# A routed front, a selective-scan mixer and a slotted expert stage in one kernel: routing order, scan entry and gate positions changed

## The chip, the cores and the metric

One NeuronCore of a Trainium2 chip runs the whole kernel. Its engines are TensorE (PE in the rows, with PEld for its weight loads), VectorE (DVE), ScalarE (ACT), GpSimd (POOL) and SyncE (SP), which here only issues DMAs. The metric is the device time of one execution in microseconds, as the median of several runs.

## The reference

A block on `x` of shape (2, 1024, 256) with a conditioning vector per batch row:

```python
c = cond(x, t_emb)            # shared SwiGLU + 8 gelu experts of width 128, top 2 by a sigmoid router, / 3
y_f = mamba(c, forward weights); y_b = flip(mamba(flip(c), backward weights))
g = sigmoid([y_f, y_b] @ gate_w + gate_b)
x = x + (g * y_f + (1 - g) * y_b) @ proj_w + proj_b
z = cond2(x, random)          # per channel: softmax over time of 2|x|/sum|x|, cumulative sum,
                              # count of sums <= random picks a time, x kept where |x| >= |x[time]|
x = x + ffn(z)                # 64 experts x 32 slots: soft dispatch over the batch, one 256x256 layer each, soft combine
```

The mixer is a Mamba layer with 512 inner channels and 16 states: a projection to `u` and `z`, a causal convolution of 4 taps and silu on `u`, a projection of it to step, B and C, `delta = softplus(dt @ dt_w + dt_b)`, and then

```python
h = exp(delta_t * A) * h + (delta_t * u_t) * B_t ;  y_t = sum_n h * C_t      # over 1024 times
y = (y + u * D) * silu(z) ;  return y @ outproj
```

## The kernel before

**Stages.** `moe_phase` computes the routed front (and folds the convolution's taps into the projection's weights on GpSimd beside it), `mamba_phase` the scan, `mix_phase` the gates, projection and thresholds, `ffn_phase` the experts. Each stage is a block in which every engine has its own program, written out by hand; semaphores order them, and nothing is reordered by a compiler. An engine works strictly in the order of its program. The products of the front and the last stage are made of three fp32r products of high and low parts (`split_products`, line 32 in the rows).

**Routing.** A unit `g` is one block of 128 hidden rows on 512 tokens: `value(g)` and `factor(g)` on TensorE into a ring of three banks, `hidden(g)` (silu or gelu) on ScalarE, `product(g)` on VectorE, `high_hidden(g)` and `low_hidden(g)` the two parts on ScalarE and VectorE, `project(g)` on TensorE. Units 0 to 3 of each 12 are the shared layer, the other eight are experts, whose factor is a gate. In the first tokens' units the router's logits are computed as well, and a chain of small VectorE operations turns them into gates: `rank`, `mask`, `den`, `rden`, `comb`, and at its end `comb_ready`. `turn_gates` on TensorE waits for it. GpSimd makes the low parts of the weights and tokens, one after the other in the order of `SPLITS`; those of the second expert weights, `rw2`, are numbers 6 and 7.

**Scan.** Four groups (2 batch rows x 2 directions) `k`, each of four channel blocks `p`: 16 periods `w` of 16 units `s`. A unit is 128 lanes (32 channels x 4 states) x 1024 times. For each, ScalarE makes `exp(delta * A)` into one of two slots of `hs` (`decay`, L1212; L1203 in the first four), GpSimd the input `dbu` (L1287), VectorE the scan (L1374) and the product with C (L1388, `weigh`), which GpSimd does for units 0, 4, 8 and 12 of most periods (L1293); TensorE sums the states of four units (`add_states`, L1087, L1080 at the very end) onto `skip`, the product with D. `hc` has six slots, `dbu` four. After unit 1 of the next period `gate_out` (L1354) multiplies the sum with `silu(z)`.

Beside this, each period makes what the next one needs: the step `t` (`step_size`, two halves of 512 times), copied by ScalarE in `step_in` (L1160, L1161), then exponential and logarithm (L1174, L1178), all ahead of a DMA that spreads it over the lanes; `z_gate` and ScalarE's `gate` (L1194), which needs another table of functions than the exponentials, so a table load before and after; and for the next group the projection `u` with its convolution and silu (`conv`, L1131). All small products share two PSUM banks in turn, in the order of `bank_uses`: a product waits until the bank's last reader is through. `pe_chores` gives TensorE's order at each quarter `r` of a period; `STEP_AT`, `GATE_AT`, `CONV_AT` and so on give the units after which ScalarE does its pieces, `LATE_STEP_AT` in the last period of a group.

**Entry into the scan.** For the first group the convolution isn't folded: ScalarE copies `u` (L1136, L1137), VectorE applies three taps (L1398), ScalarE the silu (L1142), TensorE the projection to rows of step, B and C (L966). The rows go to DRAM and come back spread over the lanes. The first four units get their step and input from PSUM by products with a spreading matrix (L999, L1009), and `replica` (L1185) copies the inputs.

**Mix.** Per batch row and channel half: magnitudes and shares on ScalarE, then on VectorE the cumulative sum (L1799) and three passes for the threshold.

## Time and profile before

| | us |
|---|---|
| runs | 1465.29, 1465.84, 1461.80; median 1465.29 |
| profiled execution | 1465.12 |
| its span | 1463.3 |
| PE busy | 1178.0 |
| DVE busy | 1150.0 |
| POOL busy | 884.2 |
| ACT busy | 771.5 |

The stages follow each other with a fence between: the front to about 184 us, the scan to 1060, the mix to 1121, the experts to the end. A row of the order of time gives start, duration, engine, line, operation, tiles and number of instructions merged into it; in brackets stands the idle time of the engine ahead of it and who ended it.

### The profile page before, as it was taken

What the parts mean: (1) busy time and instruction counts of PE and PEld (TensorE: products, weight loads), DVE (VectorE), ACT (ScalarE), POOL (GpSimd) and SP (SyncE); (2) the same over time, 40 slices, a digit from 0 to 9 for tenths busy, and PEclk for the clock granted to TensorE, in tenths of its full rate; (3) what the DMA queues carried; (4) which work ended last, traced back from release to release, by engine and by line L of the source; (5) the groups of instructions that cost most, each with busy time, mean ns of one, the idle gap of its engine ahead of it and who ended that gap; (6) DMA issues with size and microseconds to landing.
All of it is one profiled execution on the core that took longest, in us unless ns stands there. A gap on an engine that the chain in (4) does not pass through costs nothing. (4 is left out here: it accounts for less than half of the span.)

```text
span 1463.3 us, 14748 instructions
## 1 busy us (share of the span) xinstructions
PE 1178.0 (81%) x4924; PEld 651.5 (45%) x4924; DVE 1150.0 (79%) x1052; ACT 771.5 (53%) x1031; POOL 884.2 (60%) x394
## 2 busy tenths in 40 slices
PE   6999986787649887469887466484499999999998
PEld 4788732232113332113322122131147788787887
DVE  4444469999999999999999999999977754545445
ACT  5444465777545776555775555465246534333330
POOL 4420028999999999999999999999910000000000
PEclk9999998998859899769999588687699999999999
DMA  5353235341463234345123337313014130303012
GB/s 202 113 175 134 78 121 207 130 172 72 162 230 147 95 132 157 118 189 201 72 98 137 145 128 295 142 59 115 0 60 170 51 125 1 144 0 129 0 35 80
DMA packets 46016, 176.34 MB, mean 121 GB/s; under 512 B 5873, under 2 KB 10481, under 8 KB 33538
## 3 DMA queue, kind: packets, MB, share of 16 engines
q1 hardware_dynamic: 45954, 175.57, 32.7%
q8 instruction: 32, 0.52, 0.1%
q14 instruction: 30, 0.25, 0.1%
HBM read 142.78 MB, written 32.77 MB: 120 GB/s over the span
## 5 line engine op out<-in xcount | busy, mean ns | idle before, releaser
L1287 POOL TENSOR_TENSOR scan_dbu<-scan_rep,scan_bc 128x1024 f32<-128x1024 f32 x254 | 592.6, 2361 | 33.4 <-ACT scan_rep L1185 26.0
L1374 DVE TENSOR_TENSOR_SCAN scan_hs<-scan_hs,scan_dbu 128x1024 f32<-128x1024 f32 x191 | 436.7, 2286 | 11.3 <-ACT scan_hs L1212 9.9
L1212 ACT ACTIVATE scan_hs<-scan_rep,scan_neg_a 128x1024 f32<-128x1024 f32 x252 | 280.7, 1118 | 305.7 <-DVE scan_hc L1388 279.9
L1087 PE MATMUL scan_ysum<-scan_hc,scan_sel 128*32 128x512 f32 x1008 | 172.9, 818 | 210.1 <-DVE scan_hc L1388 200.0
L1388 DVE TENSOR_TENSOR scan_hc<-scan_hs,scan_bc 128x1024 f32<-128x1024 f32 x191 | 233.5, 1223 | 6.1
L1087 PEld LDWEIGHTS scan_ysum<-scan_hc,scan_sel 128*32 128x32 f32 x1008 | 36.1, 131 | 324.1 <-issue 276.0
L1293 POOL TENSOR_TENSOR scan_hc<-scan_hc,scan_bc 128x1024 f32<-128x1024 f32 x65 | 153.2, 2357 | 12.7 <-DVE scan_hc L1374 12.3
L1374 DVE TENSOR_TENSOR_SCAN scan_hc<-scan_hs,scan_dbu 128x1024 f32<-128x1024 f32 x65 | 148.1, 2278 | 0.8 <-POOL scan_dbu L1287 0.7
L947 PE MATMUL banks<-late_xin,scan_inwf 128*128 128x512 f32 x256 | 115.6, 606 | 0.0
L32 PE MATMUL ffn_sl<-ffn_tanh_s,xm_s 128*128 128x512 f32 x384 | 107.2, 415 | 2.3 <-DVE ffn_tanh_s L2169 2.3
L1989 PE MATMUL ffn_oy<-ffn_y,ffn_et 128*128 128x256 f32 x448 | 102.0, 379 | 0.8 <-DVE ffn_y L2216 0.8
L1989 PEld LDWEIGHTS ffn_oy<-ffn_y,ffn_et 128*128 128x128 f32 x448 | 84.9, 190 | 13.5 <-DVE ffn_y L2216 1.3
L32 PE MATMUL banks<-phi_s,xt_s 128*128 128x512 f32 x336 | 85.3, 400 | 0.7 <-PEq L1461 0.7
L947 PEld LDWEIGHTS banks<-late_xin,scan_inwf 128*128 128x128 f32 x256 | 48.4, 193 | 69.7 <-issue 69.7
L32 PE MATMUL moe_second<-moe_hid_s,moe_w_s 128*128 128x512 f32 x288 | 73.6, 391 | 5.2 <-DVE moe_hid_s L459 5.2
L32 PEld LDWEIGHTS ffn_sl<-ffn_tanh_s,xm_s 128*128 128x128 f32 x384 | 70.0, 190 | 16.3 <-DVE ffn_tanh_s L2169 3.3
L2084 ACT ACTIVATE ffn_lsb<-banks 128x512 f32<-128x512 f32 x56 | 33.4, 596 | 65.2 <-PE banks L32 63.8
L32 PEld LDWEIGHTS banks<-phi_s,xt_s 128*128 128x128 f32 x336 | 60.9, 188 | 13.9 <-issue 2.4
L2178 DVE TENSOR_TENSOR ffn_tanh<-ffn_lsb 128x512 f32<-128x512 f32 x24 | 16.6, 692 | 61.2 <-ACT ffn_lsb L2084 61.2
L32 PEld LDWEIGHTS moe_second<-moe_hid_s,moe_w_s 128*128 128x128 f32 x288 | 53.5, 188 | 18.3 <-DVE moe_hid_s L459 5.8
L32 PE MATMUL moe_first<-moe_x_s,moe_w_s 128*128 128x512 f32 x240 | 60.0, 391 | 0.4 <-POOL moe_w_s L417 0.4
L2075 ACT ACTIVATE ffn_et<-ffn_tb 128x512 f32<-128x512 f32 x32 | 19.0, 594 | 76.4 <-PE ffn_tb L2021 76.4
(277 smaller groups left out, 1805.3 us busy)
## 6 DMA issues: line engine op xcount, KB each, us to landing
scan_rep<-dd_rows SPq DMA_DIRECT2D x60, 1024.0 KB, 5.6
scan_bc<-bc_rows SPq DMA_DIRECT2D x32, 512.0 KB, 5.9
ffn_wt<-in_ew SPq DMA_DIRECT2D x16, 1024.0 KB, 8.0
dd_rows<-scan_dd SPq DMA_DIRECT2D x15, 1024.0 KB, 3.8
scan_bc<-gate_rows SPq DMA_DIRECT2D x24, 256.0 KB, 4.8
scan_inwf<-fold SPq DMA_DIRECT2D x12, 512.0 KB, 3.8
cond<-scan_bc SPq DMA_DIRECT2D x16, 256.0 KB, 3.0
y_all<-scan_yo SPq DMA_DIRECT2D x6, 512.0 KB, 3.1
```

What stands on the lines that cost most here:

```text
L32: mm = nc.tensor.matmul(out, lhs[x], rhs[y], start=first and i == 0, stop=last and i == 2)
L947: mm = nc.tensor.matmul(out, inwf[:, q % IWR, c, t, :], xin[k % 2][:, c, h * CT + t:h * CT + t + CT], start=(t == 0 and c == 0), stop=(t = ...
L1087: mm = nc.tensor.matmul(ysum[i * D32:(i + 1) * D32, h, :], sel[:], hc[:, (s0 + i) % HCR, h * CT:(h + 1) * CT], start=False, stop=last, til ...
L1212: nc.scalar.activation(hs[:, s % HSR, :], rep[:, e % REPS, 0, :], ACT.Exp, scale=scale).then_inc(da_done, 1)
L1287: nc.gpsimd.tensor_tensor(dbu[:, s % DBR, :], rep[:, e % REPS, 1, :], bc[:, j, 0, :], ALU.mult).then_inc(dbu_done, 1)
L1293: nc.gpsimd.tensor_tensor(hc[:, s % HCR, :], hc[:, s % HCR, :], bc[:, s % UPP // NI, 1, :], ALU.mult).then_inc(pool_hc_done, 1)
L1374: nc.vector.tensor_tensor_scan(states, hs[:, s % HSR, :], dbu[:, s % DBR, :], 0.0, ALU.mult, ALU.add).then_inc(scan_done, 1)
L1388: nc.vector.tensor_tensor(hc[:, s % HCR, :], hs[:, s % HSR, :], bc[:, r // NI, 1, :], ALU.mult).then_inc(hc_done, 1)
L1989: mm = nc.tensor.matmul(bank[:, b * DM:(b + 1) * DM], et[:, b, j, m * P:(m + 1) * P], y[:, j, b, :], start=(j == 0), stop=(j == JT - 1))
L2075: nc.scalar.activation(et[:, 0, :, m * P:(m + 1) * P], tb[:].rearrange("p (j s) -> p j s", j=JT), ACT.Copy).then_inc(et_act, 1)
L2084: nc.scalar.activation(lsb[:, m % 2, b, :], lg[:, (m + 1) % 2 if first else b, :], ACT.Copy).then_inc(l_copied, 1)
L2178: nc.vector.tensor_tensor(tanh[:], lsb[:, m % 2, 1, :], first_logits[:, m, :] if first else lsb[:, m % 2, 0, :], ALU.subtract).then_inc(di ...
```

## The change

Six things, in order of the program:

- In the routing TensorE makes five products of zeros (`IDLE_PRODUCTS`) after the first small product. On VectorE `low_hidden(2)` and `product(3)` go ahead of `mask`; on GpSimd the splits of `rw2` wait for `comb_ready`. `turn_gates` goes ahead of `value(5)`, `factor(4)` ahead of `value(6)`. ScalarE loads the silu table before the last `output`.
- The entry into the scan: the last channel block is convolved and activated in two halves; each half goes on to its projection, its copy (half 0 on ScalarE, half 1 on VectorE), its step. B rows for units 0 to 3 are spread by TensorE into `hs` slot 1 (`spread_rows`) and copied into `bc` by ScalarE, so one DMA less brings them. The input of unit 1 is spread into `ysum` and used from there. GpSimd does `weigh(0)` ahead of its inputs; `skip(0, 0)` comes after the spreads; the exponential of `neg_a` comes after the steps.
- In each period `z` comes ahead of `skip`, but in the last period of a group and the very first; `gate` comes at unit 3 instead of 4, or at 6 in those last periods (`LATE_GATE_AT`); 7 in the very first stays.
- The step's exponential and logarithm both come at unit 2 (before: 2 and 3), or 4 (before: 5).
- For periods 1 and 2 of a group's channel blocks (`split_step`) the second half of the step product moves from the end of one period into the start of the next, behind the sums. The late sigmoids go from units 9 and 14 to 10 and 15.
- In the mix each cumulative sum follows its own share.

```diff
+            pe.wait_ge(padded, 1)
+            for _ in range(IDLE_PRODUCTS):
+                zeros = comb_wide[:].rearrange("p t e -> p (t e)")
+                nc.tensor.matmul(by_expert, zeros[:, 0:P], zeros, start=True, stop=True)
...
             project(2)
+            turn_gates()
             value(5)
             project(3)
-            turn_gates()
+            factor(4)
             value(6)
-            factor(4)
...
             high_hidden(NC * UNITS - 1)
+            nc.scalar.preload_act_table_set("silu_and_others")
             output(NC - 1)
...
                 pool.wait_ge(high_done, s + 1)
+                if s == RW1:
+                    pool.wait_ge(comb_ready, 1)
...
             product(2)
+            low_hidden(2)
+            product(3)
             link(nc.vector.tensor_scalar(mask[:], rank[:], float(TOP_K), None, ALU.is_lt))
...
-            low_hidden(2)
-            product(3)
...
+def split_step(k, p):
+    return k + 1 < GROUPS and p in (1, 2)
+def gates_late(k, p):
+    return p == DC - 1 or (k, p) == (0, 0)
...
-        return [(*key, h) for key in step for h in range(HALVES)] + [("skip", k, p)] + [("z", k, p, h) for h in range(HALVES)]
+        split = [("t", k, p + 1, 1)] if split_step(k, p) else []
+        gate, own = [("z", k, p, h) for h in range(HALVES)], [("skip", k, p)]
+        return [(*key, h) for key in step for h in range(HALVES)] + split + (own + gate if gates_late(k, p) else gate + own)
...
-    step = [(*key, h) for key in step for h in range(HALVES)] if r == NJ - 1 else []
+    step = [(*key, h) for key in step for h in range(1 if split_step(k, p + 1) else HALVES)] if r == NJ - 1 else []
...
-STEP_AT = (1, 2, 3)
-LATE_STEP_AT = (3, 5, 5)
-GATE_AT, FIRST_PERIOD_GATE_AT = 4, 7
+STEP_AT = (1, 2, 2)
+LATE_STEP_AT = (3, 4, 4)
+GATE_AT, LATE_GATE_AT, FIRST_PERIOD_GATE_AT = 3, 6, 7
...
-FIRST_GATE_AT = {9: 0, 14: 1}
+FIRST_GATE_AT = {10: 0, 15: 1}
...
+            def spread_rows(h):
+                freed(pe, ("x", 0, h))
+                pe.wait_ge(consts_in, 3 * 16)
+                nc.tensor.matmul(hs[:, 1, h * CT:(h + 1) * CT], spread[0:XROWS, NI * P:], dbl[:, h * CT:(h + 1) * CT],
+                                 start=True, stop=True).then_inc(spread_done, 1)
...
+                if i == 1:
+                    for h in halves:
+                        mm = nc.tensor.matmul(ysum[:, h, :], spread[:, i * P:(i + 1) * P], dd[:, 1, h * CT:(h + 1) * CT],
+                                              start=True, stop=True)
...
+                act.wait_ge(spread_done, h + 1)
+                nc.scalar.activation(bc[:, 0, 0, h * CT:(h + 1) * CT], hs[:, 1, h * CT:(h + 1) * CT], ACT.Copy).then_inc(uc0_done, 1)
...
+                    if s == DVE_INPUTS:
+                        weigh(0)
...
+                    nc.vector.tensor_tensor_scan(cum[:, cc, :], ones[:], share[:, cc, :], 0.0, ALU.mult, ALU.add).then_inc(chain, 1)
+                    links[0] += 1
                 each(b, lambda cc, s: nc.vector.reciprocal(s[:, 1:2], s[:, 3:4]))
-                each(b, lambda cc, s: nc.vector.tensor_tensor_scan(cum[:, cc, :], ones[:], share[:, cc, :], 0.0,
-                                                                   ALU.mult, ALU.add))
```

TensorE's program in the routing, from project(1) to project(4): L32 into `moe_second` is a `project`, L32 into another tile a `value` or `factor`, L244 / L250 `turn_gates`, L284 / L290 an expert's factor. Before:

```order
L32 MATMUL moe_second<-moe_hid_s,moe_w_s 128x512 x6
L32 MATMUL moe_first<-moe_x_s,moe_w_s 128x512 x6
L32 MATMUL moe_second<-moe_hid_s,moe_w_s 128x512 x6
L32 MATMUL moe_first<-moe_x_s,moe_w_s 128x512 x6
L32 MATMUL moe_second<-moe_hid_s,moe_w_s 128x512 x6
L244 MATMUL moe_first<-moe_ident,moe_comb_wide 32x128 x16
L32 MATMUL banks<-moe_x_s,moe_w_s 128x512 x6
L284 MATMUL moe_first<-moe_gates_s,moe_ident_s 128x512 x4
L284 MATMUL banks<-moe_gates_s,moe_ident_s 128x512 x2
L32 MATMUL moe_second<-moe_hid_s,moe_w_s 128x512 x6
```

And of the change:

```order
L32 MATMUL moe_second<-moe_hid_s,moe_w_s 128x512 x6
L32 MATMUL moe_first<-moe_x_s,moe_w_s 128x512 x6
L32 MATMUL moe_second<-moe_hid_s,moe_w_s 128x512 x6
L250 MATMUL moe_first<-moe_ident,moe_comb_wide 32x128 x16
L32 MATMUL moe_first<-moe_x_s,moe_w_s 128x512 x6
L32 MATMUL moe_second<-moe_hid_s,moe_w_s 128x512 x6
L290 MATMUL moe_first<-moe_gates_s,moe_ident_s 128x512 x2
L32 MATMUL banks<-moe_x_s,moe_w_s 128x512 x6
L290 MATMUL moe_first<-moe_gates_s,moe_ident_s 128x512 x2
L290 MATMUL banks<-moe_gates_s,moe_ident_s 128x512 x2
L32 MATMUL moe_second<-moe_hid_s,moe_w_s 128x512 x6
```

`turn_gates` has moved up by a value and a project, and the first factor stands one value earlier.

TensorE's program at the border of the scan's periods 1 and 2: L947 / L980 is the folded projection, L983 / L1027 the step, L1087 / L1139 the sums, L1059 / L1111 `skip`, L1024 / L1076 `z`. Before:

```order
L947 MATMUL banks<-late_xin,scan_inwf 128x512 x8
L983 MATMUL banks<-scan_dbl,scan_dtw 128x512 x2
L1087 MATMUL scan_ysum<-scan_hc,scan_sel 32x512 x8
L1059 MATMUL scan_ysum<-late_uc,scan_diag 128x512 x2
L1024 MATMUL banks<-scan_xin,scan_inwz 128x512 x4
L1087 MATMUL scan_ysum<-scan_hc,scan_sel 32x512 x8
```

And of the change:

```order
L980 MATMUL banks<-late_xin,scan_inwf 128x512 x8
L1027 MATMUL banks<-scan_dbl,scan_dtw 128x512
L1139 MATMUL scan_ysum<-scan_hc,scan_sel 32x512 x8
L1027 MATMUL banks<-scan_dbl,scan_dtw 128x512
L1076 MATMUL banks<-scan_xin,scan_inwz 128x512 x4
L1111 MATMUL scan_ysum<-late_uc,scan_diag 128x512 x2
L1139 MATMUL scan_ysum<-scan_hc,scan_sel 32x512 x8
```

One half of the step now stands behind the sums, and `z` ahead of `skip`.

ScalarE's program from unit 0 of the scan's period 1: L1212 / L1270 is the exponential, L1160 and L1161 / L1214 and L1215 the step's copies, L1174 and L1178 / L1228 and L1232 its exponential and logarithm, L1194 / L1252 the gate. Before:

```order
L1212 ACTIVATE scan_hs<-scan_rep,scan_neg_a 128x1024
L1174 ACTIVATE scan_dd<-scan_dd 128x1024
L1212 ACTIVATE scan_hs<-scan_rep,scan_neg_a 128x1024
L1178 ACTIVATE scan_dd<-scan_dd 128x1024
L1212 ACTIVATE scan_hs<-scan_rep,scan_neg_a 128x1024
L1194 ACT_TABLE_LOAD
L1194 ACTIVATE scan_sz<-banks 128x512 x2
L1253 ACT_TABLE_LOAD
L1212 ACTIVATE scan_hs<-scan_rep,scan_neg_a 128x1024 x4
```

And of the change:

```order
L1270 ACTIVATE scan_hs<-scan_rep,scan_neg_a 128x1024
L1228 ACTIVATE scan_dd<-scan_dd 128x1024
L1232 ACTIVATE scan_dd<-scan_dd 128x1024
L1270 ACTIVATE scan_hs<-scan_rep,scan_neg_a 128x1024
L1252 ACT_TABLE_LOAD
L1252 ACTIVATE scan_sz<-banks 128x512 x2
L1316 ACT_TABLE_LOAD
L1270 ACTIVATE scan_hs<-scan_rep,scan_neg_a 128x1024 x5
```

The logarithm and the gate each stand one exponential earlier.

## Rows read from the trace of the kernel before

**Rows 1.** The page: busy time, and two groups of the scan
```profile
PE 1178.0 (81%) x4924; PEld 651.5 (45%) x4924; DVE 1150.0 (79%) x1052; ACT 771.5 (53%) x1031; POOL 884.2 (60%) x394
...
L1212 ACT ACTIVATE scan_hs<-scan_rep,scan_neg_a 128x1024 f32<-128x1024 f32 x252 | 280.7, 1118 | 305.7 <-DVE scan_hc L1388 279.9
...
L1388 DVE TENSOR_TENSOR scan_hc<-scan_hs,scan_bc 128x1024 f32<-128x1024 f32 x191 | 233.5, 1223 | 6.1
```

**Rows 2.** PE's 40 slices on the page; one stretch of the scan, columns PE to POOL
```profile
PE   6999986787649887469887466484499999999998
...
600.00:700.00 100.00, 66.53 (x219) 22.17 (x218) 97.47 (x56) 58.10 (x62) 98.10 (x44) 0.78 0.50 184
```

**Rows 3.** Order of time, TensorE, start of the routing
```profile
12.07 4.82 PE L32 MATMUL banks<-moe_x_s,moe_w_s 128*128 128x512 f32 x12 [8.05 <-DVE moe_w_s L443]
...
34.65 1.64 PE L32 MATMUL moe_second<-moe_hid_s,moe_w_s 128*128 128x512 f32 x6 [2.28 <-DVE moe_hid_s L459]
...
38.57 1.66 PE L32 MATMUL moe_second<-moe_hid_s,moe_w_s 128*128 128x512 f32 x6 [0.92 <-DVE moe_hid_s L459]
...
43.29 1.15 PE L284 MATMUL moe_first<-moe_gates_s,moe_ident_s 128*128 128x512 f32 x4 [0.47 <-issue]
...
46.23 1.62 PE L32 MATMUL moe_second<-moe_hid_s,moe_w_s 128*128 128x512 f32 x6 [1.31 <-DVE moe_hid_s L459]
```

**Rows 4.** Order of time, VectorE, the chain that makes the gates
```profile
29.00 1.74 DVE L486 TENSOR_SCALAR moe_mask<-moe_rank 128x128 f32<-128x128 f32 x1
30.77 2.36 DVE L487 TENSOR_TENSOR moe_comb_wide<-moe_prob,moe_mask 128x128 f32<-128x128 f32 x1
...
37.62 0.29 DVE L499 TENSOR_TENSOR moe_comb_wide<-moe_comb_wide,moe_mask 128x128 f32<-128x128 f32 x1
```

**Rows 5.** Order of time, entry into the scan
```profile
187.58 1.28 ACT L1230 ACT_TABLE_LOAD   x1
...
190.20 7.14 PE L956 MATMUL banks<-scan_xin,scan_inwf 128*128 128x512 f32 x16 [0.50 <-ACT late_uc L1137]
...
191.50 12.11 DVE L1398 SCALAR_TENSOR_TENSOR late_uc<-scan_hc,scan_taps,late_uc 128x1024 f32<-128x1024 f32 x9 [1.11 <-ACT late_uc L1137]
...
215.57 1.22 DVE L1366 TENSOR_TENSOR scan_dbu<-banks,scan_bc 128x1024 f32<-128x1024 f32 x1 [2.42 <-DMA scan_bc<-bc_rows]
...
228.09 2.35 POOL L1293 TENSOR_TENSOR scan_hc<-scan_hc,scan_bc 128x1024 f32<-128x1024 f32 x1
...
235.20 2.30 DVE L1374 TENSOR_TENSOR_SCAN scan_hs<-scan_hs,scan_dbu 128x1024 f32<-128x1024 f32 x1
...
253.69 2.30 DVE L1374 TENSOR_TENSOR_SCAN scan_hs<-scan_hs,scan_dbu 128x1024 f32<-128x1024 f32 x1 [1.07 <-POOL scan_dbu L1287]
```

**Rows 6.** VectorE's waits, 230 to 1070 us: total us, times, longest
```profile
DVE scan_hs L1374 <- ACT scan_hs L1212: 9.9, 18, 2.2
...
DVE late_uc L1354 <- PE scan_ysum L1087: 1.9, 2, 1.1
...
DVE wide L1354 <- PE scan_ysum L1087: 1.1, 1, 1.1
```

**Rows 7.** Order of time, ends of period 1: TensorE's sums, ScalarE's gate
```profile
314.05 1.92 PE L1087 MATMUL scan_ysum<-scan_hc,scan_sel 128*32 128x512 f32 x16 [1.43 <-DVE scan_hc L1388]
...
328.13 3.64 PE L1087 MATMUL scan_ysum<-scan_hc,scan_sel 128*32 128x512 f32 x16
...
340.20 1.08 ACT L1194 ACTIVATE scan_sz<-banks 128x512 f32<-128x512 f32 x2
```

**Rows 8.** Order of time: GpSimd's last gap, its inputs 248 to 251, scan 249
```profile
918.47 2.36 POOL L1293 TENSOR_TENSOR scan_hc<-scan_hc,scan_bc 128x1024 f32<-128x1024 f32 x1 [0.31 <-DVE scan_hc L1374]
...
1027.14 9.33 POOL L1287 TENSOR_TENSOR scan_dbu<-scan_rep,scan_bc 128x1024 f32<-128x1024 f32 x4
...
1033.52 2.27 DVE L1374 TENSOR_TENSOR_SCAN scan_hs<-scan_hs,scan_dbu 128x1024 f32<-128x1024 f32 x1
```

**Rows 9.** Order of time, VectorE in the mix, second batch row
```profile
1101.25 4.47 DVE L1799 TENSOR_TENSOR_SCAN scan_bc<-mix_ones,scan_bc 128x1024 f32<-128x1024 f32 x2
```

117 lines of the change are left out of this document (72 added, 45 removed).

## The prediction

> **What bounds the kernel now.** The page comes first: no engine is busy all the time, TensorE 81%, VectorE 79%, GpSimd 60% [rows 1], in a span of 1463.3 us. The slices and one stretch say why: there are three stages with different bounds [rows 2]. In the routing stage TensorE is at 9 tenths or more from the second slice of 36.6 us to the fifth, and so again in the last ten slices; in the scan between (217 to 1059 us) VectorE is at 97.47 of 100 and GpSimd at 98.10, with TensorE's granted clock at 0.78, that is part of the time at 1.2 instead of 2.4 GHz. The change touches the start of the routing stage, the entry into the scan, the order inside the scan's 16 periods, and one place in the mix between scan and last stage. So the third view is the order of time at these places, read for the gap of the engine that bounds the stage, since only that gap can be won, and the fourth is the list of VectorE's waits inside the scan.
>
> **Routing, first 47 us.** TensorE's work there is fixed; what can go is its gaps, 2.28 + 0.92 + 0.47 + 1.31 = 4.98 us, and slow matmuls [rows 3]. The gaps wait for the chain of small VectorE operations that ends in `comb_ready`. In it a 128x128 mask takes 1.74 us and a 128x128 product 2.36, where the same size takes 0.29 a little later [rows 4]: the long ones lie beside GpSimd's splits. The change puts `low_hidden(2)` and `product(3)` ahead of the chain and holds GpSimd's split of the second expert weights until `comb_ready`. My walk: project(2)'s operand is ready at 30.4, when TensorE is still in value(4), so the 2.28 goes; the chain starts at 31.1 instead of 29.0, but its eleven links now take 3.1 us, so `comb_ready` comes at 34.2 instead of 37.9; the gate transposes meet it with 0.3 us of waiting, and project(4) starts at 42.4 instead of 46.23 after one gap of about 1.0. So 4.98 - 0.3 - 1.0 = 3.7 us. What is late next: the held splits, 2 x 2.4 us from 34.2, end at 39 and are needed at 42.4.
> The first twelve products take 4.82 us [rows 3], where six take 1.62 and less later on: they run at the lower clock after an empty stretch of 8 us. The five products of zeros go ahead of them, in a gap of 8.05 us; they are ten instructions of such a kind as take 7.14 / 16 = 0.45 us at the higher clock [rows 5], so at half of it they would end near 13, 1 us too late, at worst. If the clock has risen midway they end near 10.4 and cost nothing. Then value(0) ends at 13.5; factor(0) waits for GpSimd's split until 14.2, and 16.82 - 15.6 = 1.2 us is won. Bounds: -1 and 1.9. Routing: **4.9 us** (2.7 to 6.9).
> The trace agrees with a rule of the Trainium skill ("SBUF — State Buffer", Who interferes with whom): a VectorE operation with two SBUF inputs and a GpSimd one block each other whole. By it the links cost what they cost alone, as I took. The skill's "TensorE: Matmul & The Clock Gate" (Part 1) has the slow state as the default that activity releases; whether zeros are activity enough no row shows.
>
> **Entry into the scan.** The table load of 1.28 us stands between ScalarE's second and third copies [rows 5] and goes to a place where ScalarE idles; VectorE's taps for the second channel block start 191.50 -> 190.75, 0.7 us. The last taps are cut in two halves (0.8 us more work), but projection, step and softplus of the first half run beside the second. B rows no longer pass through DRAM for unit 0: the 2.42 us wait for them goes; instead two more TensorE products and two ScalarE copies. My walk puts scan(0) at 213.8 instead of 215.57 + 1.22 = 216.8. Unit 1's product comes straight from PSUM, scan(1) at 217.4. GpSimd does weigh(0) first, not after inputs(3) (2.35 us) [rows 5]. Not all arrives: ScalarE now has the step's copies, exponential and logarithm ahead of decay(5), so scan(5) starts at 232.9 instead of 235.20, 2.3 us. The 1.07 us that scan(10) waits for GpSimd goes too, since that engine started 4.8 us earlier. **3.4 us** (1 to 5: below if the copies of B make decay(0) late, above if ScalarE catches up). `skip(0,0)` moves behind the spreads and is hidden: its first reader needs product 3.
>
> **Inside the scan.** VectorE waits for ScalarE's exponentials 18 times, 9.9 us, and for TensorE's sum at the period's end 1.9 + 1.1 us in three periods [rows 6]: 12.9 us, all that can be won. Why: after exponential r (1.12 us) [rows 1] the gate costs 1.28 + 1.08 + 1.28, the next exponential 1.12, together 5.9 us. From the release of exponential r to scan r+1 VectorE has two pairs of scan (2.3) and product (1.2), 6.9 us; but 5.8 if GpSimd makes one of the products, as at unit 4. There the gate ends late, mostly by 0.35 us. At unit 3 both products are VectorE's and a microsecond is over. In last periods of a group the gate waited for its product (2.24 us once); at unit 6 that is long done. Elsewhere z now precedes skip and no longer waits for VectorE's gate_out. The two sigmoid pairs move from 9 and 14 to 10 and 15, away from GpSimd's units 11 and 13.
> The three gate_out waits: in periods 1 and 2 of a group the second half of the step product waited for a bank behind a ScalarE convolution and held the sums, which then took 3.64 us at the lower clock, 1.92 at the higher [rows 7]. The split puts it behind the sums.
> What comes back: (a) in those six periods ScalarE's second step copy now waits for that half. At the higher clock the half is there in time; at the lower one it comes at about 331.2 where ScalarE wanted it at 329.6, and copies, exponential, logarithm, exponential, gate, exponential then end 1.0 us after scan(4) could start. 0 to 6 x 1.0 us; I take 0.4 each, 2.4, as the sums will mostly start earlier but still behind a gap. (b) GpSimd has 25 gaps of 0.2 to 1.1 us in the scan, some 20 us, the last of them at 918; after it none. Unit 249's input ends there at 1027.14 + 2 x 2.33 = 1031.8, its scan starts at 1033.52, a lead of 1.7 us [rows 8], while five of VectorE's waits, 2.2 us, lie after 918 and go: 0.5 is lost. **12.9 - 2.4 - 0.5 = 10.0 us** (4 to 12.9).
>
> **Mix.** Each cumulative sum starts when its own share is there instead of both (two take 4.47 us [rows 9]); 1.2 us earlier on VectorE, twice. But TensorE's projections, and then ScalarE's turned copies, end later than VectorE in both halves. **0.2 us** (0 to 1.2). The last stage is untouched.
>
> **Sum.** 4.9 + 3.4 + 10.0 + 0.2 = 18.5 us. The profiled execution took 1465.12 us, its span and 1.8 us around it, 0.2 under the median of 1465.29: 1465.1 - 18.5 = 1446.6, or 1446.7 against the median.
>
> **Rivals.**
> - *The win turns into new waits.* ScalarE late at unit 4 in all six periods by 1 us or more, and GpSimd, at 98.10 of 100, passes its own lateness on. For it: half the periods run at a clock near 0.78, and the slack is near 1 us. Against: GpSimd still has its 20 us of gaps until 918 [rows 8]. The scan then gives 4: 1452.7. Chance 0.15.
> - *Everything that is late goes*, and routing and entry reach their upper ends: 6.5 + 5 + 12.5 + 0.5 = 24.5: 1440.7. Chance 0.14.
> - *The zeros don't raise the clock and run late*: 1.2 lost and 1 more, the routing's chain behind them: 1448.9. For: no row shows a product of zeros. Against: little stands on it. By the skill's clock page, default slow and raised by activity, they do raise it, if its activity is busy time and not data. Chance 0.06.
> - *Slower: z ahead of skip delays the sums.* z waits for banks that ScalarE's step copies free, and skip and the first sums queue behind it on TensorE. Unit 6's product reuses unit 0's slot of `hc` and waits for those sums. At the lower clock z 4.8 + skip 3.8 from 331 end about when product 3 is there (340), sums at 344, and unit 6 wants them at 348.3: 4.3 us of room. It decides once z ends more than that late; at 2.5 us in each of twelve periods it costs 30 against the 18.5 won: 1476. Against: copies end before 333. Chance 0.03.
> - *Nothing measurable*: the moved gates find z not ready, and the early wins fill up before the next fence; 1461 to 1469. Every term would have to fail together. Chance 0.03.
> My forecast has 0.59; its own range is 1442 to 1451.
>
> **How the numbers follow.** Leaving out about 0.2, from 1440 to 1455: lower end, the second rival; upper end, the first with its scan term at 2. About 0.3%, 4.4 us, is what a measurement can tell from no change. Faster: 0.59 + 0.15 + 0.14 + 0.06 less a little that ends near 1461 = 0.93; same 0.04; slower 0.03.
>
> **What would show it.** Of the changed kernel: (1) first twelve L32 products in about 3 us, `comb_ready` operations of 0.2 to 0.3 us each, and TensorE without a gap from 43 us; the routing's end near 177 instead of 182. (2) No wait for the rows' DMA before the first scan; tenth unit 8 us earlier than before in all. (3) VectorE's waits for ScalarE's exponentials at most 3 us in the scan instead of 9.9, none before gate_out; if they stand at unit 4 of periods 1 and 2, (a) was undersized. (4) GpSimd's gaps before 918 fall from 20 us to about 10. The forecast is wrong if VectorE's rate per unit changes, or if TensorE's gaps in routing come back behind `comb_ready`.

## The result and the profile after

The changed kernel takes 1458.4 us in the median of nine runs (1453.71 to 1459.26), the kernel before 1465.15 of nine (1461.80 to 1467.74): ratio 0.9947, 95% interval 0.9936 to 0.9958. It is faster, by 7 us where 18.5 had been forecast, and lies outside the range of 1440 to 1455. The profiled execution took 1458.22 us, span 1456.4.

The nine runs are not one heap: 1453.7, 1453.8 and 1456.1, then six from 1458.2 to 1459.3. The trace is of the second kind. What separates the two groups comes out below; 1456.1 has no trace and stays open.

The page, to be held against [rows 1]: busy time, then the same two groups of the scan (here L1270 and L1456).

```profile
PE 1197.3 (82%) x4938; PEld 658.0 (45%) x4938; DVE 1144.4 (79%) x1056; ACT 773.8 (53%) x1032; POOL 885.1 (61%) x394
...
L1270 ACT ACTIVATE scan_hs<-scan_rep,scan_neg_a 128x1024 f32<-128x1024 f32 x252 | 281.1, 1118 | 280.1 <-DVE scan_hc L1456 235.2
...
L1456 DVE TENSOR_TENSOR scan_hc<-scan_hs,scan_bc 128x1024 f32<-128x1024 f32 x191 | 233.6, 1223 | 6.1
```

The operations cost what they cost, 1118 and 1223 ns. TensorE is busy 19.3 us longer: 14 instructions more (ten for the zeros, four for the B rows), and matmuls at the lower clock (0.892 in the mean of the span, before 0.899).

**Where the time went.** Four marks cut both traces into five stages; each is the start of one VectorE row: the first taps of the entry, scan(10) of the first period (counted from 0), the last gate_out, the first addition of the mix. All tables here use them.

| stage | before | after | won | forecast |
|---|---|---|---|---|
| start to first taps | 185.60 | 180.15 | 5.45 | 4.9 |
| taps to scan(10) | 68.09 | 71.31 | -3.22 | 3.4 |
| scan(10) to last gate_out | 804.86 | 796.92 | 7.94 | 10.0 |
| gate_out to first addition of the mix | 3.88 | 7.14 | -3.26 | 0 |
| from there to the end | 400.87 | 400.88 | -0.01 | 0.2 |

Sum: 6.90 us, and 1463.3 - 1456.4 = 6.9.

**Routing** went as told. TensorE in order of time, against [rows 3]:

```profile
3.86 6.28 PE L225 MATMUL moe_second<-moe_comb_wide 128*128 128x512 f32 x10
12.16 1.63 PE L32 MATMUL banks<-moe_x_s,moe_w_s 128*128 128x512 f32 x6 [2.02 <-DVE moe_w_s L452]
14.31 1.65 PE L32 MATMUL banks<-moe_x_s,moe_w_s 128*128 128x512 f32 x6 [0.53 <-POOL moe_w_s L426]
...
40.87 1.63 PE L32 MATMUL moe_second<-moe_hid_s,moe_w_s 128*128 128x512 f32 x6 [1.01 <-DVE moe_hid_s L468]
```

The five products of zeros, ten instructions, end at 10.1; the first twelve products of the routing take 1.63 + 1.65 instead of 4.82; project(4) starts at 40.87 instead of 46.23, behind one gap of 1.0. And VectorE's chain, against [rows 4]:

```profile
30.02 0.22 DVE L497 TENSOR_SCALAR moe_mask<-moe_rank 128x128 f32<-128x128 f32 x1
30.28 0.29 DVE L498 TENSOR_TENSOR moe_comb_wide<-moe_prob,moe_mask 128x128 f32<-128x128 f32 x1
...
32.70 0.29 DVE L508 TENSOR_TENSOR moe_comb_wide<-moe_comb_wide,moe_mask 128x128 f32<-128x128 f32 x1
```

What had taken 1.74 and 2.36 beside GpSimd takes 0.22 and 0.29. GpSimd has no operation from 29.8 to 33.1 now.

**Entry.** VectorE, against [rows 5]:

```profile
185.75 12.90 DVE L1466 SCALAR_TENSOR_TENSOR late_uc<-scan_hc,scan_taps,late_uc 128x1024 f32<-128x1024 f32 x12 [0.81 <-ACT late_uc L1186]
...
214.65 1.23 DVE L1434 TENSOR_TENSOR scan_dbu<-banks,scan_bc 128x1024 f32<-128x1024 f32 x1 [3.52 <-PE banks L1061]
...
231.07 2.29 DVE L1442 TENSOR_TENSOR_SCAN scan_hc<-scan_hs,scan_dbu 128x1024 f32<-128x1024 f32 x1 [0.50 <-ACT scan_hs L1270]
234.13 2.30 DVE L1442 TENSOR_TENSOR_SCAN scan_hs<-scan_hs,scan_dbu 128x1024 f32<-128x1024 f32 x1 [0.78 <-ACT scan_hs L1270]
```

The wait for the rows' DMA (2.42) is gone, and in its place stands one of 3.52 for TensorE. That engine:

```profile
200.24 1.09 PE L1027 MATMUL banks<-scan_dbl,scan_dtw 17*128 17x512 f32 x2 [0.86 <-ACT scan_dbl L1196]
201.26 1.46 PE L1012 MATMUL scan_hs<-scan_dbl,scan_hc 64*128 64x512 f32 x2
202.65 1.97 PE L1003 MATMUL banks<-late_uc,scan_xw 128*64 128x512 f32 x2
205.54 2.04 PE L1027 MATMUL banks<-scan_dbl,scan_dtw 17*128 17x512 f32 x2 [0.93 <-DVE scan_dbl L1469]
207.51 2.07 PE L1012 MATMUL scan_hs<-scan_dbl,scan_hc 64*128 64x512 f32 x2
```

L1027 is the step, L1012 the B rows, L1003 the x product. From the third row on two instructions take 2.0 us, not 1.0: the lower clock. It falls within the second row (1.46). The same in a stretch (its length; busy of PE, PEld, DVE, ACT, POOL; granted clock):

```profile
202.00:212.00 10.00, 9.07 (x10) 2.45 (x10) 3.55 (x6) 4.81 (x9) 0.00 (x0) 0.50 0.33 101
```

0.50 is 1.2 GHz. Before, the clock stood at 1.00 from 188 to 221.

**Scan.** VectorE's waits, 230 to 1070 us, against [rows 6]:

```profile
DVE scan_hs L1442 <- ACT scan_hs L1270: 4.5, 8, 1.1
...
DVE scan_hc L1442 <- ACT scan_hs L1270: 3.1, 4, 0.9
```

7.6 us instead of 9.9, of which 1.3 are the two entry rows above; no wait before gate_out, which had been 3.0 (the last gate_out of all waits 2.0 in both traces and is not counted). The 6.4 us behind unit 10, from the order of time: units 2 and 4 of periods 2 and 9 and unit 4 of period 10 (0.46, 0.88; 0.24, 0.88; 0.87), the last group's periods 12 and 14 (0.70, 1.14, 0.86), and two of 0.2. One of them, and the half of the step product that it comes from:

```profile
338.96 2.29 DVE L1442 TENSOR_TENSOR_SCAN scan_hc<-scan_hs,scan_dbu 128x1024 f32<-128x1024 f32 x1 [0.88 <-ACT scan_hs L1270]
```
```profile
328.94 0.60 ACT L1214 ACTIVATE scan_dd<-banks 128x512 f32<-128x512 f32 x1 [1.91 <-PE banks L1027]
```

**Behind the scan** three engines meet at the fence. TensorE, and then GpSimd:

```profile
1046.44 1.90 PE L1132 MATMUL scan_ysum<-scan_hc,scan_sel 128*32 128x512 f32 x4 [1.32 <-DVE scan_hc L1456]
1051.75 5.37 PE L1648 MATMUL mix_pp<-late_uc,scan_inwf 128*128 128x512 f32 x8 [3.41 <-PEq L728]
```
```profile
1046.61 4.63 POOL L1379 TENSOR_TENSOR late_uc<-late_uc 128x1024 f32<-128x1024 f32 x2
```

VectorE's gate_out ends at 1048.38 + 1.22 = 1049.6, GpSimd at 1051.24; before, at 1059.77 and 1059.86, together. TensorE stands still for 3.41 us instead of 1.85, and its first eight products take 5.37 us instead of 3.67. From the last gate_out to the end of the span it is 408.0 us, before 404.75.

### The profile page after: what moved, and what is told of

Its sections match the earlier page's. It is cut to its first block and busy times, and to the rows that moved or that the text cites. A ratio compares the mean times of both kernels' runs of the same rounds, so it can differ in the third digit from the quotient of the medians.

```text
span 1456.4 us, 14779 instructions
## 1 busy us (share of the span) xinstructions
PE 1197.3 (82%) x4938; PEld 658.0 (45%) x4938; DVE 1144.4 (79%) x1056; ACT 773.8 (53%) x1032; POOL 885.1 (61%) x394
## 3 DMA queue, kind: packets, MB, share of 16 engines
q1 hardware_dynamic: 45810, 175.11, 33.1%
## 5 line engine op out<-in xcount | busy, mean ns | idle before, releaser
L1270 ACT ACTIVATE scan_hs<-scan_rep,scan_neg_a 128x1024 f32<-128x1024 f32 x252 | 281.1, 1118 | 280.1 <-DVE scan_hc L1456 235.2
L1139 PE MATMUL scan_ysum<-scan_hc,scan_sel 128*32 128x512 f32 x1008 | 176.2, 832 | 223.5 <-DVE scan_hc L1456 206.3
L1456 DVE TENSOR_TENSOR scan_hc<-scan_hs,scan_bc 128x1024 f32<-128x1024 f32 x191 | 233.6, 1223 | 6.1
L1139 PEld LDWEIGHTS scan_ysum<-scan_hc,scan_sel 128*32 128x32 f32 x1008 | 36.0, 132 | 334.6 <-issue 293.8
L980 PE MATMUL banks<-late_xin,scan_inwf 128*128 128x512 f32 x256 | 117.1, 612 | 0.0
L32 PE MATMUL ffn_sl<-ffn_tanh_s,xm_s 128*128 128x512 f32 x384 | 106.1, 411 | 3.1 <-DVE ffn_tanh_s L2239 3.1
L32 PE MATMUL banks<-phi_s,xt_s 128*128 128x512 f32 x336 | 85.3, 401 | 0.7 <-PEq L1531 0.7
L980 PEld LDWEIGHTS banks<-late_xin,scan_inwf 128*128 128x128 f32 x256 | 49.0, 196 | 72.2 <-issue 72.2
L32 PEld LDWEIGHTS ffn_sl<-ffn_tanh_s,xm_s 128*128 128x128 f32 x384 | 69.3, 188 | 16.9 <-DVE ffn_tanh_s L2239 4.2
L32 PE MATMUL moe_second<-moe_hid_s,moe_w_s 128*128 128x512 f32 x288 | 73.3, 390 | 1.7 <-DVE moe_hid_s L468 1.7
L32 PEld LDWEIGHTS banks<-phi_s,xt_s 128*128 128x128 f32 x336 | 60.9, 188 | 13.9 <-issue 2.4
L32 PE MATMUL moe_first<-moe_x_s,moe_w_s 128*128 128x512 f32 x240 | 60.1, 391 | 0.4 <-POOL moe_w_s L426 0.4
L32 PEld LDWEIGHTS moe_second<-moe_hid_s,moe_w_s 128*128 128x128 f32 x288 | 53.8, 188 | 13.9 <-POOL moe_x_s L426 1.4
```

The costliest lines, as they stand in the source:

```text
L32: mm = nc.tensor.matmul(out, lhs[x], rhs[y], start=first and i == 0, stop=last and i == 2)
L980: mm = nc.tensor.matmul(out, inwf[:, q % IWR, c, t, :], xin[k % 2][:, c, h * CT + t:h * CT + t + CT], start=(t == 0 and c == 0), stop=(t = ...
L1139: mm = nc.tensor.matmul(ysum[i * D32:(i + 1) * D32, h, :], sel[:], hc[:, (s0 + i) % HCR, h * CT:(h + 1) * CT], start=False, stop=last, til ...
L1270: nc.scalar.activation(hs[:, s % HSR, :], rep[:, e % REPS, 0, :], ACT.Exp, scale=scale).then_inc(da_done, 1)
L1456: nc.vector.tensor_tensor(hc[:, s % HCR, :], hs[:, s % HSR, :], bc[:, r // NI, 1, :], ALU.mult).then_inc(hc_done, 1)
```

## The experiments

Times are medians; the interval is that of the ratio to the kernel before, measured beside each (1464.2 to 1465.7). In the table: taps, entry (taps to scan(10)), scan (to gate_out), fence (to the mix's first addition), as above, then TensorE's granted clock at the entry, between 198 and 214 us.

| kernel | us | ratio | taps | entry | scan | fence | clock at entry |
|---|---|---|---|---|---|---|---|
| before | 1465.15 | | 185.60 | 68.09 | 804.86 | 3.88 | 1.00 |
| changed | 1458.4 | 0.9936-0.9958 | 180.15 | 71.31 | 796.92 | 7.14 | 0.50 for 10 us |
| routing_alone | 1458.2 | 0.9943-0.9969 | 180.16 | 68.17 | 803.12 | 4.41 | 1.00 |
| old_entry | 1454.9 | 0.9911-0.9936 | 180.16 | 67.12 | 796.62 | 7.21 | 1.00 |
| order_alone | 1459.5 | 0.9955-0.9977 | 185.84 | 67.09 | 796.73 | 7.14 | 1.00 |
| no_zeros | 1458.6 | 0.9951-0.9976 | 182.48 | 68.58 | 797.79 | 7.08 | 0.50 for 3 us |
| six_zeros | 1454.3 | 0.9914-0.9967 | 180.10 | 66.93 | 797.53 | 7.14 | 1.00 |
| four_zeros | 1457.9 | 0.9934-0.9967 | 180.46 | 66.92 | 796.49 | 7.13 | 1.00 |
| entry_fill | 1453.8 | 0.9917-0.9945 | 180.11 | 66.93 | 796.87 | 6.91 | 1.00 |
| longer_gap | 1462.4 | 0.9972-0.9998 | 180.15 | 74.96 | 797.59 | 7.14 | 0.50, twice |
| entry_order | 1452.6 | 0.9910-0.9938 | 180.04 | 64.82 | 796.87 | 6.91 | 1.00 |
| end_fill | 1454.3 | 0.9915-0.9946 | 180.32 | 66.96 | 796.68 | 5.45 | 1.00 |
| end_share | 1456.6 | 0.9933-0.9960 | 180.02 | 71.36 | 794.54 | 4.90 | 0.50 for 10 us |
| no_split | 1455.9 | 0.9930-0.9958 | 180.16 | 71.39 | 794.53 | 6.90 | 0.50 for 10 us |
| all_mended | 1449.0 | 0.9885-0.9917 | 180.15 | 64.84 | 793.31 | 4.41 | 1.00 |
| mended_no_fill | 1449.6 | 0.9889-0.9924 | 180.13 | 64.82 | 793.32 | 4.90 | 1.00 |
| mended_end1 | 1450.1 | 0.9853-0.9934 | 180.09 | 68.14 | 794.84 | 4.36 | 0.50 for 7 us |
| all_rows | 1449.6 | 0.9888-0.9919 | 180.14 | 66.55 | 793.13 | 6.89 | 1.00 |
| mended_all_rows | 1444.3 | 0.9850-0.9886 | 180.26 | 64.64 | 792.33 | 4.40 | 1.00 |
| before_rows | 1460.0 | 0.9961-0.9983 | 186.07 | 67.27 | 800.39 | 3.78 | 1.00 |

The column of times is of all executions, the stage columns are of one execution each. Kernels whose scan is the same (changed, old_entry, order_alone, no_zeros, six_zeros, four_zeros, entry_fill, longer_gap, entry_order, end_fill) differ by up to 1.3 us in it, and end_share, whose periods are also the same but for the last, lies 2 us below them. Behind the mix's first addition the rest takes 400.8 to 401.2 us, but 402.1 in end_share and mended_no_fill and 402.0 in old_entry: there a part of the loss stands behind the last mark.

### The parts by themselves

`routing_alone` is the kernel before with the hunks of the routing (lines 57 to 505 of the kernel, the table load excepted), `order_alone` the kernel before with the hunks on `pe_chores`, `STEP_AT`, `GATE_AT`, `split_step` and `FIRST_GATE_AT`, `old_entry` the changed kernel without the hunks of the entry.

Of the routing's hunks, for one:

```diff
+            for _ in range(IDLE_PRODUCTS):
...
+                if s == RW1:
+                    pool.wait_ge(comb_ready, 1)
```

> The kernel before with the routing's edits alone (products of zeros, low_hidden(2) and product(3) ahead of the mask, GpSimd's splits held until comb_ready, turn_gates and factor(4) earlier). In the changed kernel the routing stage ended 5.3 us earlier. Theory A (each stage passes its gain on): the scan starts 5.3 us earlier and so does the end, 1465.2 - 5.3 = 1459.9, and the conv products, the first scan and the last gate_out all stand 5 to 5.5 us before those of the kernel before. Rival B (GpSimd or the rows' DMA bounds what follows, and an early start is partly given back): the shift is smaller at the first scan or at the last gate_out than at the routing's end, and the time 1461 to 1464.

> The changed kernel with the entry into the scan of the kernel before (everything else changed). In the changed kernel scan(10) came only 2.2 us earlier though 5.4 us were in hand, so the new entry seems to lose 3.2 us. Theory A: with the old entry scan(10) stands 5.3 us earlier than before, and the time is 1458.4 - 3.2 = 1455.2. Rival B (GpSimd is the bound of the whole scan from here on, and its start decides): its first input starts at about 217 instead of weigh(0) at 218.35, so 1 to 1.5 us are won, 1457. Rival C: the new entry is worth its predicted 3.4 us and something else is lost: 1461.8.

And of `order_alone`:

```diff
-STEP_AT = (1, 2, 3)
+STEP_AT = (1, 2, 2)
...
-GATE_AT, FIRST_PERIOD_GATE_AT = 4, 7
+GATE_AT, LATE_GATE_AT, FIRST_PERIOD_GATE_AT = 3, 6, 7
```

> The kernel before with the order inside the scan's periods alone (z ahead of skip, gate at unit 3 or 6, exponential and logarithm together, the split step, the late sigmoids). Theory A: from scan(10) to the last gate_out 8 us are won, as in the changed kernel, and of these 2 to 3.3 are lost at the fence behind the scan, where GpSimd ends later than VectorE: 1465.2 - 8 + 2.7 = 1460. Rival B (the order wins what was predicted, 10, when it starts from the old entry): 1457 to 1458. Rival C (the scan's gain in the changed kernel was in part the routing's, since waits shifted against the DMAs): under 5 us in the scan, 1462 to 1463.

The routing's 5.4 us arrive whole at the entry (theory A), and 1.7 more come in the scan, where VectorE waits 8.2 us for exponentials and not 9.9. It isn't chance of one execution alone: four of the five runs lie between 1457.8 and 1458.5, 7 us under the kernel before. Its cause is open. By itself the routing thus gives as much as the whole change (1458.2 and 1458.4): in the median nothing is left of the other parts. `order_alone` shows the order by itself: 8.1 us won in the scan, 3.3 of them lost at the fence, which is the changed kernel's ledger without its routing. `old_entry` is 3.5 us faster than the changed kernel with everything of the new entry taken out: so the new entry cost time in the median. The five runs, 1451.2 to 1455.3, have the clock at 1.00 in the one that was traced.

`no_zeros`:

```diff
-        IDLE_PRODUCTS = 5
+        IDLE_PRODUCTS = 0
```

> The changed kernel without the five products of zeros at the start. Theory A (they raise the clock for the first six products of value(0), predicted at 1.2 us): value(0) and factor(0) take 4.8 us for twelve products again, the logits start 1.0 to 1.2 us later, and comb_ready, the first x projection and the end all come about 1 us later. Rival B (the split of the weights on GpSimd bounds factor(0), the rest is absorbed behind comb_ready): the start is later but the end of the routing is not. Rival C (the clock rises by itself): nothing changes.

TensorE in order of time without the zeros:

```profile
12.23 5.46 PE L32 MATMUL banks<-moe_x_s,moe_w_s 128*128 128x512 f32 x12 [8.28 <-DVE moe_w_s L452]
```

The last link to `comb_ready` (VectorE's addition) starts at 34.66 instead of 32.70, and the taps 2.3 us later. Theory A, but the zeros are worth 2.3 us, twice the 1.2 of the sum. The medians can't be set against each other for this: how many of the runs have the lower clock at the entry differs.

### The entry: clock or order

`entry_fill`:

```diff
             def first_x_proj():
+                fill(2)
...
                                      start=False, stop=True).then_inc(out[h][1], 1)
+                    fill(1, CT // 2)
                     step_size(0, 0, h)
```

`fill(n, cols)` repeats a product of `inwf` and `xin` into `ysum`, which is overwritten later.

> The changed kernel with five more products on TensorE in the gaps of the entry, whose result is never read: two of 128x512 before the first x projection, and one of 128x256 behind the last x product of each half. In the changed kernel TensorE ran at a granted clock of 0.50 from 201.7 to 212.2 us, behind gaps of 1.8 and 0.9 us; the kernel before has gaps of 1.7 and 0.4 there and stays at 1.00. Theory A (the gaps let the clock fall, and the clock cost the entry its gain): the clock stays at 1.00 from 192 to 216, step and spread products take 1.0 us for two instead of 2.0, scan(0) starts 3.5 to 4.5 us earlier than in the changed kernel, and the time is 1454.5 to 1455.5. Rival B (it is the order: x products of half 1 queue behind step and spread of half 0 whatever the clock): the clock stays up but scan(0) is at most 1.5 us earlier, 1457. Rival C (products of 17 and 64 rows let the clock fall, not the gaps): the clock falls near 202 as before, and the time is 1458.4 plus 0.5 to 1 for the added products.

`longer_gap`:

```diff
                 out = [claim(("x", 0, h)) for h in range(HALVES)]
+                pe.wait_ge(uc0_done, DC - 1)
```

> The changed kernel, in which TensorE waits with the first x projection until the silu of the third channel block is through (at about 194.9), so that its gap ahead of these products is 3.5 us instead of 1.8. Theory A (the gap decides whether the clock falls in the entry): all executions have the lower clock from within the x products on, scan(0) at 218 or later, and the time is 1 to 3 us above the 1458.4 of the changed kernel's slower group; none is near 1453.8. Rival B (chance, or the rows of the later products): two groups as before, each about 1.7 us later than in the changed kernel.

`entry_fill` looked like a clean win for theory A: five of six runs at 1453.7 to 1454.7, clock 1.00. It was none: the trace of `end_fill`, with the changed kernel's entry untouched, also had the clock at 1.00 and scan(0) at 211.8. And `longer_gap` spoke against the gap: two runs at 1457.7 and eight at 1460.7 to 1463.8, the changed kernel's two groups, each some 4 us later, where theory A wanted one. In its trace the clock fell twice: behind the lengthened gap of 3.67 us, where the first twelve x products, of 128 rows, took 7.03 us instead of 5.33, and again near 206, behind the first step and B rows. So a gap can do it too. The next two kernels leave the entry as it is and give two more traces of it.

`six_zeros`, and `four_zeros` with 4:

```diff
-        IDLE_PRODUCTS = 5
+        IDLE_PRODUCTS = 6
```

> The changed kernel with six products of zeros instead of five. Theory A (only the clock matters, and it has risen by the fifth): the first six products of value(0) take 1.63 us as with five, comb_ready stays at 32.7; and the profiled execution, if near 1453.8, has TensorE's clock at 1.00 throughout 198 to 214, if near 1458.4, at 0.50 for about 10 us of it, with 4 to 4.6 us between the two at scan(0). Rival B (the groups differ inside the scan or at its end): scan(0) at 216 in both.

> The changed kernel with four products of zeros instead of five. Theory A: the four end about 1 us earlier than five, the gap ahead of value(0) grows from 2.0 to about 2.5 us, and value(0) still runs at the higher clock: no change in comb_ready. Rival B: it is the last product that raises the clock, and value(0) and factor(0) take 4.8 us again as in no_zeros, comb_ready at 34.7. For the two groups as with six_zeros.

Both profiled executions were of the faster kind (1454.3 and 1453.7). six_zeros, the stretch shown above for the changed kernel:

```profile
202.00:212.00 10.00, 9.07 (x20) 3.27 (x20) 5.23 (x8) 6.32 (x11) 0.00 (x0) 1.00 0.49 156
```

The same 9.07 us busy, but twenty instructions instead of ten; scan(0) at 211.5 instead of 216.0. The two groups are the clock at the entry, worth 4.4 us. It can also fall for a shorter time: in no_zeros it was at 0.50 for some 3 us behind 207, and the entry took 68.58. `value(0)` takes 1.63 us with four, five or six products of zeros.

`entry_order`:

```diff
+                for h in range(HALVES):
                     step_size(0, 0, h)
+                for h in range(HALVES):
                     spread_rows(h)
...
             first_silu(DC - 1, 0, 1)
-            first_rows(0)
             first_silu(DC - 1, 1, HALVES)
+            first_rows(0)
```

> The changed kernel with another order at the end of the entry: ScalarE does the second half's silu ahead of the first half's rows, and TensorE makes both halves' step products ahead of both halves' B rows (before: step and B rows of half 0, then x product, step and B rows of half 1). In the changed kernel the second silu was free to start at 198.65 and started at 200.00, and the last x product stood behind step and B rows of half 0. Theory A (the order of the halves cost the entry its predicted gain, beside the clock): where TensorE runs at its higher clock there, scan(0) starts at 209.4 instead of 211.6, the last x product follows the first directly, and the time is 2 us under the changed kernel's at the same clock, 1451.8; where it runs at the lower, 1456. Rival B (scan(0) is bound by the B rows or by GpSimd's start): scan(0) earlier, scan(10) not, 1453.8. Rival C: the two step products wait for the rows of half 1 and hold nothing else back, so nothing changes.

Theory A, and to the tenth: VectorE's first scan, and ScalarE's second silu ahead of the rows.

```profile
209.38 2.29 DVE L1444 TENSOR_TENSOR_SCAN scan_hc<-scan_hs,scan_dbu 128x1024 f32<-128x1024 f32 x1
```
```profile
198.58 0.63 ACT L1194 ACTIVATE late_uc<-late_uc 128x512 f32<-128x512 f32 x1 [1.83 <-DVE late_uc L1468]
199.30 0.68 ACT L1198 ACTIVATE scan_dbl<-banks,scan_one_row 64x512 f32<-64x512 f32 x1
```

The entry takes 64.8 us instead of 66.9 at the same clock. Against the old one, 67.1 to 68.2 as the rows' DMA falls, it now wins 2.3 to 3.4; with the changed kernel's order it was 0.2 to 1.2 even at the higher clock. Of the five runs two lie at 1451.1 and 1451.6 and one at 1455.7, as expected for the two clocks; 1452.6 and 1453.4 lie between.

### The end of the scan

`end_fill`, behind the last `add_states`:

```diff
+            for _ in range(3):
+                nc.tensor.matmul(hs[:, 0, 0:CT], ident[:], hc[:, 0, 0:CT], start=True, stop=True)
```

> The changed kernel with three products of 128x512 on TensorE behind the scan's last sums, whose result is never read. In the changed kernel TensorE stands still for 3.4 us there, since the fence waits for GpSimd until 1051.2, and its first eight products of the mix take 5.37 us; before it stood still for 1.85 us and they took 3.67. Theory A (the longer gap lets the clock fall): the eight take 3.6 us, the first addition in the mix comes 1.7 us earlier, and 1456.7. Rival B (the clock was low for what ran before the gap): they still take over 5 us, 1458.4. Rival C: the mix has another bound, and the 1.7 us are given back before the last stage, 1458.4 with fast products.

`end_share`, VectorE ahead of the last gate_out (GpSimd's loop loses these two, and its last sum waits for them):

```diff
+                if w == PERIODS - 1:
+                    dve.wait_ge(late.dif_first, KC)
+                    for h in range(HALVES):
+                        own = late.y_first[:, KC - 1, h * CT:(h + 1) * CT]
+                        nc.vector.tensor_tensor(own, own, late.gate_first[h][KC - 1], ALU.mult).then_inc(late.dif_first, 1)
```

> The changed kernel, in which VectorE makes the last two of the four gate products (128x512) that GpSimd had at the scan's end, in the 2.0 us in which VectorE waits for TensorE's last sums. In the changed kernel GpSimd ended at 1051.24 and VectorE's gate_out at 1049.60, and the mix began behind the later of the two. Theory A (GpSimd's end sets the fence, 1.6 us of the lost gain): GpSimd ends 2.5 us earlier, before VectorE; the mix's first addition comes 1.6 us earlier against gate_out, and, as TensorE's gap before the mix falls from 3.4 to 1.8 us, its first eight products take 3.7 us instead of 5.4: 3.3 us in all, 1458.4 to 1455.1 in executions with the lower clock at the entry and 1453.8 to 1450.5 in the others. Rival B (DMA or fence itself): under 0.5 us.

end_fill, then end_share, TensorE's first products in the mix:

```profile
1047.34 3.67 PE L1650 MATMUL mix_pp<-late_uc,scan_inwf 128*128 128x512 f32 x8 [0.65 <-PEq L728]
```
```profile
1048.22 5.37 PE L1656 MATMUL mix_pp<-late_uc,scan_inwf 128*128 128x512 f32 x8 [2.34 <-PEq L728]
```

With the gap filled the eight are fast, 1.7 us, theory A. With the gap shortened to 2.34 they are not. The fence column falls from 7.14 to 4.90, but VectorE's second addition then waits 2.06 us instead of 0.89:

```profile
1053.63 0.75 DVE L1857 SCALAR_TENSOR_TENSOR scan_xin<-mix_pp,late_prb,scan_xin 128x512 f32<-128x512 f32 x1 [2.06 <-PE mix_pp L1656]
```

From the last gate_out to the end it is 408.0 us in the changed kernel, 407.0 in end_share, 406.3 in end_fill, 405.3 in all_mended, which has both, and 404.75 before. So of the 3.3 us lost 1.7 are the clock and 1.0 came back by sharing; 0.55 stay. GpSimd did not end ahead of VectorE either: its last sum waited 1.23 us for VectorE's product and ended at 1047.7, gate_out at 1047.1. The 2.4 us that end_share's profiled execution wins in the scan are mostly waits for exponentials (4.2 us behind scan(10), changed kernel 6.4), which the edit does not touch.

The length of the stop alone does not decide about the clock. In routing_alone:

```profile
1053.79 3.67 PE L1586 MATMUL mix_pp<-late_uc,scan_inwf 128*128 128x512 f32 x8 [2.37 <-PEq L707]
```

### The split

`no_split`:

```diff
-    return k + 1 < GROUPS and p in (1, 2)
+    return False
```

> The changed kernel without the split of the step product: both halves of the step product stand at the end of the period before, as in the kernel before. Everything else of the new order stays. Theory A (the split takes the three waits before gate_out, 3.0 us, and gives ScalarE's lateness in the periods behind it, 3.3 us, so it is worth nothing): VectorE's waits for exponentials fall from 6.4 to about 3 us in the scan, three waits of 0.9 to 1.1 us before gate_out come back, and the time is within 0.5 us of the changed kernel's at the same clock of the entry. Rival B (the split is worth its 3 us): 3 us above, 1461.4 and 1456.8. Rival C (the waits of the periods behind it have another cause): the exponentials' waits stay at 6 us and the gate_out waits come back, 3 us above.

The scan takes 794.53 us instead of 796.92: without the split the waits for exponentials fall from 7.6 to 2.8 us (2.3 and one of 0.5), and those before gate_out come back at 1.7 only (a third, of 0.8, stands before a product of VectorE in period 14). VectorE's waits, 230 to 1046:

```profile
DVE scan_hs L1442 <- ACT scan_hs L1270: 2.3, 4, 1.1
DVE late_uc L1421 <- PE scan_ysum L1139: 1.7, 2, 1.1
```

Theory A in its mechanism, but the balance is against the split, by 2.4 us. Both traces have the lower clock at the entry, and their times, 1455.6 and 1458.2, say the same. The size is less sure than the sign: end_share, with the split, also took 794.54 in the scan in its one trace. But all five runs without it, 1455.3 to 1457.3, lie under the changed kernel's slower group.

### All together, and the rows

`all_mended` is `entry_order`, `no_split` and `end_share` in one, with `fill(2)` ahead of the first x product and two products as in `end_fill`:

```diff
+                fill(2)
...
+            for _ in range(2):
+                nc.tensor.matmul(hs[:, 0, 0:CT], ident[:], hc[:, 0, 0:CT], start=True, stop=True)
```

> The changed kernel with what the experiments before this one pointed at, all together: the halves' order at the end of the entry, no split of the step product, VectorE's share of the last gate products, two unread products of 128x512 on TensorE ahead of the first x projection and two behind the scan's last sums. Theory A (the losses are separate and add up): scan(0) at 209.4 and scan(10) at 244.9; from there to the last gate_out 794.3 us (no_split 794.5); from gate_out to the mix's first addition 3.3 us (4.9 in end_share, less 1.7 for products at the higher clock); then 400.9 us as in every run so far. Span 1443.4, time 1445.2, that is about what had been forecast for the changed kernel. Rival B (what one mends another takes: GpSimd, which has few gaps left, bounds the scan once VectorE waits less): the scan takes 796.5 or more, 1447.5 or more, and VectorE waits for GpSimd's inputs.

> The same without the four unread products. Theory A (the clock falls at the entry because of gaps in TensorE's work, and at the mix because of the gap ahead of it): at the entry the new order alone has closed the gaps behind 193, so the higher clock holds there in most executions; at the mix the first eight products take 5.4 us instead of 3.6 behind a gap of 2.3, and the time is 1.7 us above the one with the products. Rival B: the entry's gap of 1.8 us is enough to let the clock fall in some executions, which then lose 3 to 4 us more. Rival C: no difference.

The profiled execution of `all_mended` came at 1445.4, the other five at 1448.4 to 1450.6. The first meets the sum of 1445.2, in part by luck: the scan took 1.0 us less than the 794.3 of the sum, and the fence 4.41 instead of 3.3, as the sum had left out what end_share loses behind the last mark. `mended_no_fill` leaves out both fills: at the entry nothing changes, at the mix the eight products take 5.37 again, and 1445.3 against 1443.6 of span; the medians, 1449.6 and 1449.0, don't tell them apart. For the five, `mended_end1`, against `all_mended`:

```diff
-            for _ in range(2):
+            for _ in range(1):
```

> all_mended with one unread product behind the scan's last sums instead of two. Theory A (the 3.6 us between its executions lie at the entry, where the clock falls in some of them): in the profiled execution, if near 1449, TensorE's clock is 0.50 somewhere between 198 and 214 and scan(0) comes after 211. Rival B (they lie at the mix, where the clock behind the gap is low in some executions): scan(0) at 209.5, and the mix's first products slow, 3 us or more later against gate_out. Rival C (inside the scan, in waits for ScalarE): scan(0) at 209.5 and more than 794 us from scan(10) to gate_out. One product instead of two leaves a gap of about 1.3 us ahead of the mix: at most 1.7 us if the clock falls.

Its profiled execution took 1450.1, and theory A holds: scan(0) at 212.75 instead of 209.5. Two stretches:

```profile
193.00:202.00 9.00, 8.95 (x21) 2.61 (x20) 5.92 (x8) 4.84 (x7) 0.00 (x0) 1.00 0.00 0
203.00:209.00 6.00, 6.00 (x8) 1.99 (x7) 2.90 (x5) 3.30 (x7) 0.00 (x0) 0.50 0.54 197
```

TensorE had been busy 8.95 of 9 us, and its clock fell nonetheless. So at the entry it can fall without a gap. What the engine was doing from 200.3 on is step and B rows, products of 17 and 64 rows:

```profile
202.32 3.25 PE L1019 MATMUL scan_hs<-scan_dbl,scan_hc 64*128 64x512 f32 x4
```

The last experiments give them all 128 rows, zero weights and zero data added, at the same columns.

`all_rows`:

```diff
-        self.dtw = self.dtw_wide[0:DTR + 1]
+        self.dtw = self.dtw_wide[:]
...
-        dbl = sb("dbl", [XROWS, SEQ])
+        dbl = sb("dbl", [P, SEQ])
...
-                nc.tensor.matmul(hs[:, 1, h * CT:(h + 1) * CT], spread[0:XROWS, NI * P:], dbl[:, h * CT:(h + 1) * CT],
+                nc.tensor.matmul(hs[:, 1, h * CT:(h + 1) * CT], spread[:, NI * P:], dbl[:, h * CT:(h + 1) * CT],
...
-                nc.tensor.matmul(out, dtw[:, k % 2, dc * P:(dc + 1) * P], dbl[0:DTR + 1, h * CT:(h + 1) * CT],
+                nc.tensor.matmul(out, dtw[:, k % 2, dc * P:(dc + 1) * P], dbl[:, h * CT:(h + 1) * CT],
```

> The changed kernel, in which the step products (17 rows) and the products of the B rows (64 rows) take all 128 rows of the array, the added ones being zero weights or zero data; the same columns, gaps and order. Theory A (products of few rows let the clock fall): no execution falls at the entry: scan(0) at 211.6 to 211.9, and all times near 1453.8, with none at 1458 to 1459. Rival B (the gaps, or the run's timing, whatever the rows): two groups as before, five or six of ten at 1458 to 1459. Rival C: the clock of the whole scan rises as well (0.75 to 0.86 in the stretches of it), and TensorE's pieces get earlier: below 1453.

> all_mended with the same change of rows. Theory A: all executions near 1445.4 to 1446, where all_mended had one at 1445.4 and five at 1448.4 to 1450.6, and scan(0) at 209.5. Rival B: the share of slower executions stays as it was, with a median near 1449.

all_rows, TensorE, with the gaps as they were:

```profile
204.11 1.10 PE L1028 MATMUL banks<-scan_dbl,scan_dtw 128*128 128x512 f32 x2 [0.93 <-DVE scan_dbl L1473]
205.04 1.02 PE L1012 MATMUL scan_hs<-scan_dbl,scan_hc 128*128 128x512 f32 x2
```

Five runs from 1449.0 to 1450.8 instead of nine from 1453.7 to 1459.3, and four from 1444.1 to 1445.4 instead of six from 1445.4 to 1450.6: one group each. The memset and the waits that the edit adds move nothing at the entry (scan(0) at 211.4, six_zeros 211.5). Which of the two kinds of product does it, 17 or 64 rows, is not separated. Theory A and, with it, rival C: the scan itself takes 793.13 us instead of 797.53 (six_zeros, same clock at the entry). Behind the first step half in the six split periods the sums take 1.92 us in five, where the changed kernel had three at 2.69 to 3.29. ScalarE's lateness there shrinks to one wait of 0.88, in the one period that still has slow sums (3.53). The clock between 217 and 1040 us is 0.85 in the mean, changed kernel 0.82: with 128 rows it still falls elsewhere, as behind the scan, where the eight products took 5.13 us after a stop of 3.39.

> The kernel before, with all 128 rows for its step products (17 rows before; it has no products of B rows). Theory A (few rows cost at the changed kernel's entry and, by late step halves, in its split periods; the kernel before has neither place): the clock at its entry was 1.00 already, VectorE waited 0.35 us at unit 5 for a reason that the clock has no part in, and only the three waits before gate_out (3.0 us) can go: 1462 to 1465.2. Rival B (the higher clock in the scan pays everywhere): GpSimd or VectorE runs ahead, 5 us or more are won, 1460 or less.

The same edits without the B rows, on the kernel before: 1460.0, where the kernel before, measured beside it, had 1464.5. The time lies at rival B's bound, 2 us under theory A's range; what goes is mostly theory A's. All three waits before gate_out of [rows 6] are gone, 3.0 us; those for exponentials are 8.9 instead of 9.9. The sums behind the step at the start of period 5, before and with all rows:

```profile
485.66 3.64 PE L1087 MATMUL scan_ysum<-scan_hc,scan_sel 128*32 128x512 f32 x16
```
```profile
482.67 1.92 PE L1088 MATMUL scan_ysum<-scan_hc,scan_sel 128*32 128x512 f32 x16
```

At the starts of periods 1, 2, 5, 6, 9 and 10 the sums were slow (3.36 to 3.64) in five of six, with all rows in one (3.53). So of the 15.6 us between the kernel before and `all_rows` some 5 belong to the rows alone, and at equal rows the change is worth 10.4.

`mended_all_rows`, 1444.3 us, is faster than both kernels: 1.3% under the one before.

## Why the prediction was wrong

- **Routing, 4.9, measured 5.45.** The walk held in kind. Inside it the zeros were undersized (2.3 for 1.2, the bound had been 1.9) and the gaps oversized (3.1 for 3.7), so part of the hit is luck. The rule on two SBUF inputs that the prediction cites fits the 128x128 product, which has two; but the mask and the addition ahead of the reciprocal (L494), with one tensor input each, had waited too and fell from 1.74 to 0.22 and from 1.33 to 0.17.
- **Entry, 3.4, measured -3.2.** The step that failed is "projection, step and softplus of the first half run beside the second", in two ways. (i) The walk let the second half start when its taps were through. But ScalarE had the first half's rows ahead of the second silu (200.0 instead of 198.6), and TensorE step and B rows of the first half ahead of the last x product: 2.1 us, which entry_order brings back. (ii) It took TensorE's products at the higher clock. The kernel before had 1.00 there, but the change had added products of a kind that the old entry hardly had. 4.4 us in the slower executions. Together 6.5 of the 6.6 missed. In the faster ones only (i) is lost, and the two fastest, 1453.7 and 1453.8, lie inside the stated range. The prediction weighed the clock for the zeros and for (a), not here.
- **Scan, 10.0, measured 7.9.** (a) was sized 2.4 and came to 3.3 in three periods, at the unit named and two units before it; its condition, the lower clock, was right: in the 10 us from the start of the six split periods on the clock was 0.66, 0.66 and 0.83 in the three with waits and 1.00 in the three without. The last group's waits had been counted as won: 3.2 us before, 2.7 remain. (b), 0.5 for GpSimd's lead, did not come: VectorE waits for none of its inputs behind unit 3. VectorE's gain is 1.4 us more than the waits in the list explain. Some 0.8 of it, by an estimate from the same rows, is in how they are listed: without a wait two scans start 2.21 us apart, while ahead of a listed wait the earlier one fills 2.28 to 2.30, and 11 listed waits stand behind scan(10) where there were 22. The rest is open.
- **Fence, 0, measured -3.3.** Missing from the sum. The prediction read that GpSimd has no gap behind 918 [rows 8] and asked only who waits for its inputs. It does six more operations behind its last product, and ends the stage. With VectorE 10.2 us ahead and GpSimd 8.6, the difference of 1.6 was lost, and TensorE's slow products behind the longer stop cost the other 1.7.
- **Mix, 0.2, measured 0.0.** As said, TensorE ends later than VectorE there.
- **Rivals.** None had the time. The first, new waits, has the right kind for scan and fence. The third fell: zeros do raise the clock. Of the signs, (1) held; (2) half, no DMA wait but the tenth unit 2.2 us earlier and not 8; (3) failed in size, in the place that the text had named for (a); (4) GpSimd's waits for VectorE behind 230 fell from 19.0 to 15.0, not to 10.

By the Trainium skill's "TensorE: Matmul & The Clock Gate" (Part 1), the slow clock is the default, and a busy TensorE is released from it. For the zeros the trace agrees. For the entry it doesn't: in mended_end1 the engine was busy without a gap and the clock fell, and in all_rows, with the gaps left in and 128 rows, it stayed up. Behind longer stops the trace agrees again: after each of 3.38 to 3.42 us ahead of the mix eight products took 5.13 to 6.58 us. The measurement decides.

## What to carry to other kernels

An operation that a change adds on TensorE is to be priced at both clocks, and where a small product can be given all rows with zeros at no cost in columns, try it early: it was worth 8.8 us in the changed kernel and 4.5 in the one before, where the whole change had won 6.7. When a walk lets two halves overlap, go through each in-order engine's program and write down what of the other half stands ahead. And when the engine that bounds a stage gains, look for the engine with the fewest gaps and follow it to the fence, past the last thing that anyone waits for.

## What the runs showed of the hardware

- Products of 17 and 64 rows, though they keep TensorE busy, let its granted clock fall to 0.50 in some executions of the same kernel: in six of thirteen traces of the new entry, once (mended_end1) without a gap. With 128 rows it fell there in neither of two traces, and the nine times lie in one group for each kernel. In the four traces of the old entry, which has only the four instructions of the step with 17 rows, it did not fall. That the rows alone do it, whatever else runs, is not shown.
- Products whose operands are all zero raise the clock: behind four, five or six of them six instructions take 1.63 us, without them twelve take 5.46.
- Behind a stop of 3.38 to 3.42 us ahead of the mix eight products took 5.13 to 6.58 us in all eleven traces that have one, all_rows among them; behind stops of 0.45 to 1.85 they took 3.67. At 2.34 and 2.35 (end_share, mended_no_fill) they took 5.37, at 2.37 (routing_alone) 3.67.
- A table load on ScalarE took 1.28 us every time.
- A VectorE scan of 128x1024 starts 2.21 us after the one before it if nothing is waited for; a listed wait costs some 0.08 us more than the idle time shown.
